# Shared expert macro tiles inside the last attention steps of a pre-norm transformer layer kernel

## The reference, cut to what matters

```python
x = x + attn(layernorm(x), Wqkv, Wout)          # 16 heads, window 64, rope
xf = layernorm(x).reshape(-1, 128)
shared = (silu(xf @ sg) * (xf @ su)) @ sd       # sg, su: 128x256, sd: 256x128
# router: top 4 of 8 groups by cosine score, top 4 of the 32 experts in them,
# softmax of the 4 scores; each expert takes its first 640 pairs (capacity)
h = silu(buf @ wg) * (buf @ wu); out_e = h @ wd # per expert, hidden size 256
routed[token] += gate * out_e[its slot]
x = x + shared + routed
```

## Time and profile before

| what | value |
|---|---|
| median of three runs | 727.87 us (726.16 to 729.05) |
| span of the profiled execution | 904.6 us |
| PE busy | 724.0 us (80% of the span) |
| DVE busy | 534.0 us (59%) |
| POOL busy | 415.1 us (46%) |
| ACT busy | 360.9 us (40%) |
| attention, to the first early macro tile | 0 to 539.3 us |
| early macro tiles, to the first expert transpose | 539.3 to 552.9 us |
| experts, to the last down product on PE | 552.9 to 837.4 us |
| last stage | 837.4 to 904.6 us |

### The profile page before, as it was taken

The page is one execution under the profiler, slowest core; times in us unless marked ns, Lnnn a source line. Parts: engine busy times, 40 slices in busy tenths (PEclk is TensorE's granted clock), DMA queues, the critical chain, the costliest instruction groups (busy, mean ns, idle before and its releaser), DMA issues.

```text
span 904.6 us, 24570 instructions
## 1 busy us (share of the span) xinstructions
PE 724.0 (80%) x7521; PEld 563.5 (62%) x7521; DVE 534.0 (59%) x2192; ACT 360.9 (40%) x853; POOL 415.1 (46%) x548
## 2 busy tenths in 40 slices
PE   3798888988978788898888858888888888877960
PEld 1565656665646565575665637777777777777540
DVE  3476756556577676656666656545454454543598
ACT  4465544454455445444454423332323232322200
POOL 4125343353343434334344350555555555556555
PEclk9698776676798878767788859999999999998985
DMA  8991000000000000000000002423233333421355
GB/s 268 358 390 35 14 20 15 12 23 12 12 22 10 20 9 15 10 7 14 6 7 6 6 8 84 125 76 105 76 114 107 114 115 103 126 75 32 122 182 167
DMA packets 52338, 68.37 MB, mean 76 GB/s; under 512 B 9505, under 2 KB 31807, under 8 KB 52304
## 3 DMA queue, kind: packets, MB, share of 16 engines
q1 hardware_dynamic: 38240, 53.56, 18.4%
q0 software_dynamic: 9216, 11.97, 4.4%
q10 hardware_dynamic: 4848, 2.40, 0.9%
HBM read 34.89 MB, written 39.99 MB: 83 GB/s over the span
## 4 chain that ended last, share of the span: by engine, by line
PE 52%; another core or an unknown queue 19%; issue 10%; DVE 10%; ACT 6%; POOL 1%; ACTq 1%; DVEq 1%; POOLq 0%
PE bank L693 9%; PE bank L864 7%; PE bank L680 6%; PE bank L674 5%; PE bank L663 5%; PE bank L657 3%; PE bank L701 3%; DVE x_all L1246 3%; DVE mx L1044 2%; PE bank L733 2%; ACT hact L607 2%; PE bank L817 2%; PE bank L756 1%; PE bank L747 1%
## 5 line engine op out<-in xcount | busy, mean ns | idle before, releaser
L463 POOL DMA_INDIRECT pair_results<-yout,yidx x160 | 157.2, 982 | 143.4 <-ACT yout L625 104.0
L447 POOL DMA_INDIRECT expert_slots<-xfe,sidx x128 | 127.0, 992 | 141.5 <-DVE sidx L1148 108.3
L864 PE MATMUL bank<-xgT_parts,wgu_parts 128*128 128x320 f32 x768 | 147.2, 344 | 46.4 <-ACT hact L607 46.4
L864 PEld LDWEIGHTS bank<-xgT_parts,wgu_parts 128*128 128x128 f32 x768 | 125.9, 208 | 57.3 <-ACT hact L607 50.3
L519 ACT ACTIVATE pt<-bank 128x512 f32<-128x512 f32 x128 | 76.2, 596 | 182.2 <-PE bank L680 164.9
L1259 DVE TENSOR_TENSOR hact<-hact,bank 128x320 f32<-128x320 f32 x128 | 57.1, 481 | 140.2 <-ACT hact L607 133.1
L1044 DVE TENSOR_REDUCE mx<-bank 128x4 f32<-128x512 f32 x128 | 87.3, 683 | 32.5 <-PE bank L663 19.7
L421 POOL TENSOR_TENSOR pout<-pin,mhalf 128x3 f32<-128x3 f32 (+2 forms) x36 | 29.9, 830 | 127.4 <-DVE pin L970 127.4
L890 PE MATMUL bank<-wdn,hact 128*128 128x128 f32 x640 | 82.7, 288 | 2.3 <-issue 2.3
L890 PEld LDWEIGHTS bank<-wdn,hact 128*128 128x128 f32 x640 | 82.5, 207 | 2.5 <-issue 2.5
L623 ACT COPY yout<-bank 128x512 f32<-128x512 f32 x32 | 18.7, 585 | 162.2 <-remote 151.0
(11 more groups left out here) (148 smaller groups left out, 1335.1 us busy)
## 6 DMA issues: line engine op xcount, KB each, us to landing
expert_slots<-fill SPq DMA_DIRECT2D x32, 322.5 KB, 6.5
xg<-expert_slots SPq DMA_DIRECT2D x32, 322.5 KB
pair_results<-rload SPq DMA_DIRECT2D x32, 256.0 KB
rload<-pair_results SPq DMA_DIRECT2D x16, 512.0 KB, 4.0
wgu<-in_L_ffn_wg_dram SPq DMA_DIRECT2D x32, 128.0 KB
wgu<-in_L_ffn_wu_dram SPq DMA_DIRECT2D x32, 128.0 KB
wdn<-in_L_ffn_wd_dram SPq DMA_DIRECT2D x32, 128.0 KB
pair_results<-yout,yidx POOLq DMA_INDIRECT x160
```

The source lines that it names most:

```text
L447: g.indirect_dma_start(out=slots_d, out_offset=bass.IndirectOffsetOnAxis(ap=sidx[:, tr.b, k:k + 1], axis=0), in_=xfe[:, tr.b, k, :], in_of ...
L463: g.indirect_dma_start(out=pairs_d, out_offset=bass.IndirectOffsetOnAxis(ap=yidx[:, c, j:j + 1], axis=0), in_=yout[:, c, j, :], in_offset= ...
L864: last = mm(bank[2 + 2 * w + h][:, 0:CH], wgu_parts[:, e.b, wp, w, h * P:(h + 1) * P], xgT_parts[:, e.b, xp, ch * CH:(ch + 1) * CH], start ...
```

## The change

Macro tiles 0 to 5 are issued inside steps 33, 34 and 35, two per step (`drain_macro(tau, i)` gives macro tile 2(tau-33)+i). Macro tiles 6 and 7 follow the attention steps as 0 and 1 did before. The last stage holds only the 16 combines, in one loop. In the drain, gate and up have one PSUM bank each (0 and 1) and down has bank 5, where the early tiles have two each.

```diff
-    SHARED_EARLY = 2
+    SHARED_DRAIN = 6
-    COMB_EARLY = 4 * (N // 512 - SHARED_EARLY - 2)
...
+        def drain_macro(tau, i):
+            if isinstance(tau, int) and NT < tau < NT + 4:
+                return tile_of(tau - NT - 1, i)
+            return None
```

In ACT's step and behind the attention steps:

```diff
+                def drain_silu(i, h):
+                    m = drain_macro(tau, i)
+                    if m is not None:
+                        act.wait_ge(S.sh_gu, 4 * m.n + (2 * h + 1))
+                        wait(act, S.sh_down, m.n - 1)
+                        a.activation(sact[:, m.b, h], bank[0][:, :], ACT.Silu).then_inc(S.sh_act, 1)
...
+                drain_silu(0, 0)
                 if tf is not None:
...
+                drain_silu(0, 1)
                 if tw is not None:
...
+                drain_silu(1, 0)
                 exponentials(0)
...
                 exponentials(3)
+                drain_silu(1, 1)
...
-            shared_steps(shared_step, 0, SHARED_EARLY)
+            shared_steps(shared_step, SHARED_DRAIN, N // 512)
...
-            shared_steps(shared_step, SHARED_EARLY, N // 512)
```

In PE's step:

```diff
+                def drain_gate_up(i, h):
...
+                    pe.wait_ge(S.xfT_kept, 4 * m.n + 4)
+                    wait(pe, S.sh_act, 2 * m.n + h)
+                    mm(bank[0][:, :], sgw[:, cols], xfT_all[:, bass.ts(m.n, 512)], start=True, stop=True)\
+                      .then_inc(S.sh_gu, 1)
+                    wait(pe, S.sh_mul, 2 * m.n + h)
+                    mm(bank[1][:, :], suw[:, cols], xfT_all[:, bass.ts(m.n, 512)], start=True, stop=True)\
+                      .then_inc(S.sh_gu, 1)
+                def drain_down(i):
...
+                    pe.wait_ge(S.sh_mul, 2 * m.n + 2)
+                    wait(pe, S.sh_added, m.n)
+                    for j in range(4):
+                        for h in range(2):
+                            last = mm(bank[5][:, j * D:(j + 1) * D], sact[:, m.b, h, j * P:(j + 1) * P], sdw[:, h, :],
+                                      start=(h == 0), stop=(h == 1))
+                    last.then_inc(S.sh_down, 1)
```

In DVE's step and last stage:

```diff
+                def drain_times(i, h):
...
+                        dve.wait_ge(S.sh_act, 2 * m.n + (h + 1))
+                        dve.wait_ge(S.sh_gu, 4 * m.n + (2 * h + 2))
+                        v.tensor_tensor(sact[:, m.b, h], sact[:, m.b, h], bank[1][:, :], ALU.mult)\
+                         .then_inc(S.sh_mul, 1)
+                def drain_add(i):
...
+                        dve.wait_ge(S.sh_down, m.n + 1)
...
                 at(tr, masked_a)
+                drain_times(0, 0)
                 at(tp, maxima, 0)
                 at(tr, masked_b)
+                drain_times(0, 1)
...
                 at(tr, marks_b)
+                drain_times(1, 0)
...
+                drain_add(0)
                 at(tr, positions_a)
...
                 at(tr, slots_c)
+                drain_times(1, 1)
+                drain_add(1)
...
-            shared_steps(shared_and_combine, SHARED_EARLY, N // 512)
-
             dve.wait_ge(S.sh_added, N // 512)
-            for q in range(COMB_EARLY // 2, NR):
-                combine(q, q % (NR // 2), q // (NR // 2))
-            with dve.Fori(0, NT // NR - 2) as i:
+            with dve.Fori(0, NT // NR) as i:
                 for c in range(NR // 2):
-                    combine((NR // 2) * i + (NR + c), c, i + 2)
+                    combine((NR // 2) * i + c, c, i)
```

More of the change, by code:

```diff
@@ L753, in step @@
                     first_scores(0)
+                drain_gate_up(1, 0)
                 if tw is not None:
@@ L785, in step @@
                     second_scores(3)
+                drain_gate_up(1, 1)
                 if tr is not None:
@@ L849, in shared_step @@
                     last.then_inc(S.sh_down, 1)
-            shared_steps(shared_step, 0, SHARED_EARLY)
-            pe.wait_ge(S.sh_added, SHARED_EARLY)
+            pe.wait_ge(S.sh_act, 2 * SHARED_DRAIN)
+            pe.wait_ge(S.sh_mul, 2 * SHARED_DRAIN)
+            shared_steps(shared_step, SHARED_DRAIN, N // 512)
+            pe.wait_ge(S.sh_added, N // 512)
             def expert_step(en, e, ed):
```

36 lines of the change are left out of this document (24 added, 12 removed).

## The result

The changed kernel takes 747.03 us (median of four runs, 745.4 to 748.62) against 727.01 us before (median of four, 723.26 to 729.05): a ratio of 1.029, with a 95% interval of 1.025 to 1.034. It is 20 us slower. The profiled execution of the changed kernel spans 746.8 us and itself took 748.62 us. The experiments ran on four chips, numbered 1, 4, 7 and 10, and on each the kernel before takes about 900 us; so every experiment is compared with runs of the kernel before on its own chip. The first profile of before spans 904.6 us, and I take it to come from a chip of that kind, though neither its chip nor that of these runs is known. Ratios and their intervals leave out executions slowed by a state of the chip, so a ratio can differ from the quotient of the two medians beside it.

A forecast was written before the change was run, and what follows sets the result against it. PE's in-order list was taken to bound the drain, DVE and POOL the last stage. +26.6 us to the first expert less 7.9 in the last stage made +18.7, taken as +17: 745 us, range 733 to 766.

The forecast's parts named there:

- To the first expert: Drain and the stretch behind it: macro tiles there make the first expert start 26.6 us later, bounds +13 to +51.
- step 33: Drain step with 1.6 us of idle PE: +8.8 us for two macro tiles, +1.3 for a table load, sum +10.1.
- Step 34: Drain step: +6.1 as in step 35, +0.8 for L747 and L756, +2.9 for the next tile's transpose; sum +9.8.
- Step 35: Last drain step: router +1.2 us later, position count +4.9 us later behind the router; sum +6.1.
- Its last part, behind the drain: From last position count to first expert: macro tile 6 starts 2.9 us later, a faster clock gives back 2.3 us.
- The table loads: ACT in the drain: one Exp load in step 33 costs 1.3 us, the other five stand in waits and cost nothing.
- The last stage: Combines without macro tiles: 7.9 us shorter, from -7.4 for the combines and at most 0.5 for an earlier start.
- the -7.4 us of the combines: Last stage: all 16 combines at 2.71 us each take 43.4 in place of 50.8 us.
- Rival 3: Last stage: combines get no faster because of the port DVE and POOL share; +26.6 us alone, 749 to 754.5 us; chance 0.09.
- The scale: Whole kernel: +18.7 us on the profiled 904.6 us becomes +15.0 to +18.7 in runs of 727.87 us; +17 taken.
- The clock at its lower level throughout: Drain: PE's clock stays at 1.2 GHz, +46 us, or +37 in scale, 765 to 774 us; chance 0.17.
- The rival on the other side: Faster: PE packs the drain without gaps (+13), combines run at POOL's pace (-17); 724 us; chance 0.12 with no change.

The follow-up runs named there:

- after_again: The changed kernel, unchanged, on a chip where the kernel before takes about 900 us: 936.38 us beside 909.67 us, a ratio of 1.028.
- exp_for_silu: The changed kernel with Exp in place of Silu for macro tiles 0 to 5, removing six table loads: 918.87 us beside 898.29 us for the kernel before, ratio 1.025.
- act_weighs: The kernel before with POOL's last-stage multiplications moved to ACT and the adds to DVE: 887.82 us beside 901.19 us, a ratio of 0.993.
- before_again: The kernel before, unchanged, profiled a second time: a ratio of 1.010 to itself, a span of 905.2 us.

## Why the prediction was right

The forecast was 745 us in a range of 733 to 766; measured were 747.03. The sign, the mechanism and the larger term hold; the smaller term, the last stage's gain, was mis-sized, and that the scale between 900 and 727 us came out is luck.

*To the first expert: +26.6 us forecast, 26 to 28 us measured* (64.1 and 65.6 against 38.0). By parts, on chips of the first profile's kind: step 33 took 20.3 us in after_again (520.73 to 541.03) against 11.4 and 10.5 in the profiles of before, +9 to +10 where +10.1 were forecast; in the changed kernel's own first profile it took 23.2 us, at a clock of 0.85 in place of 1.00. Step 34 took 15.6 against 7.0 and 6.4 us, +8.5 to +9 for +9.8. Step 35 took 10.9 us to its last position count against 5.1, +5.9 for +6.1; from router to position count it was 9.1 us, as the steps through PE's list had it. Those are the terms that came from rows and from the order of the lists.

*Its last part, behind the drain: +2.9 - 2.3 forecast, +1.5 to +2.4 measured* (17.3 against 14.9 and 15.8). Macro tile 6 starts 4.8 us (changed kernel, 452.86 to 457.65) and 5.5 us (after_again) behind the position count, where macro tile 0 started 1.5 us behind it: +3.3 and +4.1 for +2.9. The term lacked that the down product ahead of it would run partly at the lower clock, behind a wait of 2.2 us: it took 2.62 and 3.38 us, and macro tile 6's first product 1.91 and 1.38. From there to the first expert it is 12.5 and 11.8 us against 13.5 and 14.4, so 1 us of the 2.3 came back in the changed kernel's own profile, and 1.8 to 2.6 us in after_again.

*The table loads.* +1.3 us for the one in step 33 is confirmed by exp_for_silu, whose step 33 is 1.28 us shorter, and the other five cost nothing that shows. The extra 1.4 us that the Trainium skill (ScalarE: Activation LUTs, "What ACT_TABLE_LOAD costs") would have added by its drain behind the load is not there; the exponential starts 0.01 us behind a load of 1.28 us.

*The last stage: -7.9 us forecast, -1.5 to -4.5 us measured.* The term that was mis-sized is the -7.4 us of the combines, and the step that failed is "so the macro tiles' DVE work simply adds up there". I had divided 21.6 us by 8 in the half with macro tiles and found the same 2.7 us as in the half without, and read from it that nothing was hidden. But combines that run with no macro tile from the start take 2.91 us in the changed kernel, and 46.5 us together (45.6 in after_again) in place of 50.8: -4.3 where -7.4 were forecast. A piece costs DVE 0.05 to 0.26 us more of its own time there than with macro tiles (2.76 to 2.84 against 2.58 and 2.71 us). Rival 3 was half right: DVE's combines wait for POOL's operations, as act_weighs shows. That the macro tiles' operations, which read PSUM and were never stretched, took part of that time for nothing fits these numbers, but no run isolates it. The Trainium skill's rule (SBUF — State Buffer, "SBUF: two separate sides"), one exclusive port for GpSimd and for VectorE with two SBUF inputs, agrees with the longest single operations, 1202 ns with POOL and 353 without. I had given this rival 0.09.

*The scale.* I took 17 between 15.0 and 18.7 us, with the belief that the profiler lengthened the execution, which the section on time and profile says too. It does not: the changed kernel's profiled execution took 748.62 us, and before_again's 907.02 us among runs of 897.83 to 909.04. The measured terms, +26 to +28 less 1.5 to 4.5, make 22 to 26 us where the kernel before takes 900, beside 26 us by the ratio. In the runs of the result the difference is 20 us, not the 17 that were forecast. The last stage's gain alone, set 3 to 6 us too high, accounts for that much; how the terms shrink from 900 to 727 us no run shows, since the kernel before has no profile at 727 us. That the scale I took for a wrong reason did no harm is luck.

*The rivals.* The clock at its lower level throughout (0.17) did not come: it was at 0.85 in step 33 and at 0.96 to 1.00 behind. The rival on the other side failed on both its legs; PE did not pack the drain (3.7 us idle in step 34), and the combines got slower by piece, not faster.

*What the profile was to show.* Position count near 564 us and first experts near 579 us: 567.5 and 584.8 in after_again, whose drain begins 6.3 us later than that of the first profile. Steps of 21, 17 and 12 us: 20.3, 15.6 and 10.9. Combines of 43 us: 46.5. A clock above 0.8 in the drain: 0.85 to 1.00 in its steps. Eight table loads: eight. Experts of 284 us: 282.9 in after_again, but 212.1 in the changed kernel's first profile.

## What to carry to other kernels

Idle time of an in-order engine is not room: what is put into it also stands ahead of the short instruction for which another engine waits, so compare the new work with the idle time of each step, then walk the one chain through the lists. Work taken out of a stage gives back only what did not run in other waits, and an engine that is "busy" for 95%, as DVE was in the 46.5 us of combines, may be waiting inside its instructions: compare the mean of a group with its minimum. Where it is far above, look first for another engine that works on the same memory at that time; here moving that engine's work to an idle third engine made the last stage 8 to 11 us shorter, and moving the macro tiles cost 20 us.

## What the runs showed of the hardware that I had not expected

The same program, the kernel before, takes 727 us in the runs of the result and about 900 us on each of the four chips of the experiments. That the chip makes the difference is likely, but it is not shown, since the chip of the first runs is not known. Two things differ in the traces. The granted clock in attention is 1.00 in the changed kernel's first profile (above) and 0.83 here, in before_again:

```profile
300.00:320.00 20.00, 16.45 (x220) 11.04 (x216) 13.03 (x68) 9.23 (x23) 8.75 (x14) 0.83 0.05 17
```

And ACT and SP go on late behind PE's down product of an expert. First before_again, then the changed kernel, where L939 is the down product and L638 ACT's copy of its result:

```profile
703.91 2.39 PE L890 MATMUL bank<-wdn,hact 128*128 128x128 f32 x20
...
709.59 0.58 ACT L623 COPY yout<-bank 128x512 f32<-128x512 f32 x1 [5.49 <-remote]
709.64 0.38 SPq L312 DMA_DIRECT2D wdn<-in_L_ffn_wd_dram  x1
```

```profile
603.39 2.39 PE L939 MATMUL bank<-wdn,hact 128*128 128x128 f32 x20
...
605.82 0.59 ACT L638 COPY yout<-bank 128x512 f32<-128x512 f32 x1 [2.23 <-PE bank L939]
...
605.81 0.38 SPq L317 DMA_DIRECT2D wdn<-in_L_ffn_wd_dram  x1
```

In the one, PE's 20 calls end by the trace at 706.30, and ACT and SP, which both wait for them, go at 709.6. In the other they end at 705.78 and ACT and SP go at 705.8. In before_again ACT waits in this way 28 times, 143.3 us in all, and four times more for PE, 15.2 us; in the changed kernel's first profile its waits at that copy come to 73.5 us. That is 85 us more, and the experts take 285 us, not 212. What holds the signal up, or whether the calls themselves end later than the trace has them, the traces don't tell, and no run here was made to find out. Nor is there a profile of the kernel before at 727 us, so how its drain and last stage look then stays open.
